# Writing each distance table to DRAM in two halves, in a two-layer attention and expert kernel

## The reference

```python
scores = jnp.einsum('bhqd,bhkd->bhqk', q, k) / scale
c2p_att = jnp.einsum('bhqd,hpd->bhqp', q, pos_k)
c2p = jnp.take_along_axis(c2p_att, c2p_pos, axis=-1)
p2c_att = jnp.einsum('bhkd,hpd->bhkp', k, pos_k)
p2c = jnp.swapaxes(jnp.take_along_axis(p2c_att, p2c_pos, axis=-1), -1, -2)
scores = scores + (c2p + p2c) / scale
probs = jax.nn.softmax(scores, axis=-1)
ctx = jnp.einsum('bhqk,bhkd->bhqd', probs, v)
```

## Time and profile before

| | |
|---|---|
| median of 3 runs | 2723.02 us (2717.69 to 2724.69) |
| the profiled execution | 2727.48 us |
| its span | 2725.4 us |
| mean granted clock of TensorE | 0.847 of full speed |
| busy share of the span | PE 72%, DVE 60%, ACT 38%, POOL 33% |
| DMA | 456.40 MB, mean 167 GB/s over the span |

### The profile page before, as it was taken

One profiled execution on the slowest core, in us unless ns is written; L12 is line 12 of the kernel. 1 busy time (PEld: TensorE's weight loads), 2 busy tenths in 40 slices (PEclk: granted clock), 3 DMA queues, 4 the chain that ended last, 5 costly groups with the idle time before them and its releaser, 6 DMA issues. The chain is left out here.

```text
span 2725.4 us, 47318 instructions
## 1 busy us (share of the span) xinstructions
PE 1965.8 (72%) x13556; PEld 1445.9 (53%) x13557; DVE 1632.0 (60%) x4103; ACT 1046.4 (38%) x2098; POOL 898.0 (33%) x1079
## 2 busy tenths in 40 slices
PE   6867777777777777777769999755335159999742
PEld 3435666666666666665646666433225028877421
DVE  8946665666666566665765553577747754444344
ACT  3445554555555555555423223332001163333000
POOL 4122222222222222222232220267630015554656
PEclk9979898998988888888979999777565559999876
DMA  4679998998999899999742110000001414447333
GB/s 149 195 238 287 278 290 262 290 280 271 284 266 281 255 281 269 276 280 282 233 122 62 48 30 1 0 0 0 0 19 47 178 32 155 154 148 139 109 97 110
DMA packets 290039, 456.40 MB, mean 167 GB/s; under 512 B 38608, under 2 KB 225024, under 8 KB 289824
## 3 DMA queue, kind: packets, MB, share of 16 engines
q1 hardware_dynamic: 269344, 398.77, 48.6%
q0 software_dynamic: 16320, 42.39, 6.3%
q10 hardware_dynamic: 4160, 12.58, 1.2%
HBM read 236.67 MB, written 216.92 MB: 166 GB/s over the span
## 5 line engine op out<-in xcount | busy, mean ns | idle before, releaser
L935 DVE CUSTOM_DVE_ANT_0 probs<-bank,c2p 128x512 f32<-128x512 f32 x512 | 351.8, 687 | 425.7 <-PE bank L832 217.9
L893 ACT ACTIVATE probs<-probs,neg_max 128x512 f32<-128x512 f32 x512 | 371.5, 726 | 69.9 <-DVE neg_max L935 69.5
L908 ACT COPY a_stage<-bank 128x320 f32<-128x320 f32 (+1 forms) x512 | 211.9, 414 | 427.1 <-PE bank L801 416.3
L944 DVE COPY probsT<-bank 128x512 f32<-128x512 f32 x512 | 351.2, 686 | 11.0 <-PE bank L842 10.6
L842 PE MATMUL bank<-ident,probs 128*128 128x128 f32 x2048 | 334.7, 289 | 1.0 <-ACT probs L893 0.9
L813 PE MATMUL bank<-tab,k 96*128 96x320 bf16 (+1 forms) x512 | 165.0, 322 | 197.1 <-DVE b_stage L887 149.6
L842 PEld LDWEIGHTS bank<-ident,probs 128*128 128x128 f32 x2048 | 277.3, 152 | 13.1 <-issue 1.8
L771 POOL COPY end_c2p<-a_stage 128x4 f32<-128x4 f32 (+1 forms) x128 | 24.8, 194 | 752.0 <-ACT a_stage L908 596.9
L2122 POOL DMA_INDIRECT p_x_tile<-y_d,p_token x160 | 153.0, 956 | 329.4 <-POOLq L1813 207.4
L832 PE MATMUL bank<-ident,p2c 128*128 128x128 f32 x1280 | 249.1, 296 | 0.0
L827 PE MATMUL bank<-k,q 96*128 96x384 bf16 (+1 forms) x512 | 167.3, 327 | 91.7 <-DMA p2c<-p2c_d 66.2
(11 more groups left out here) (254 smaller groups left out, 3770.0 us busy)
## 6 DMA issues: line engine op xcount, KB each, us to landing
p2c_d<-b_stage SPq DMA_DIRECT2D x64, 640.0 KB, 4.9
c2p_d<-a_stage SPq DMA_DIRECT2D x64, 640.0 KB, 4.5
p2c_d<-b_stage SPq DMA_DIRECT2D x64, 576.0 KB, 5.2
c2p_d<-a_stage SPq DMA_DIRECT2D x64, 576.0 KB, 3.5
p2c<-p2c_d SPq DMA_DIRECT2D x256, 144.0 KB, 4.5
c2p<-c2p_d SPq DMA_DIRECT2D x256, 144.0 KB, 4.3
o_sorted_d<-p_o_pair SPq DMA_DIRECT2D x80, 256.0 KB
k<-k_stack_d SPq DMA_DIRECT2D x192, 64.0 KB
```

Of the source, the lines that this page charges most:

```text
L893: act.activation(probs[:, w % 2, j, :], probs[:, w % 2, j, :], ACT.Exp, bias=neg_max[:, w % 2, j:j + 1], scale=-1.0).then_inc(exp_done, 1)
L908: act.copy(staged(a_stage, wa % 2, wa % TPB)[:, j, :], bank[A_BANK][:, 0:width(wa % TPB)]).then_inc(a_copied, 1)
L935: dve.tensor_tensor_reduce(probs[:, w % 2, j, :], bank[S_BANKS[(HB * w + j) % 3]][:], c2p[:, w % 2, j, :], -SCALE, LOWEST, ALU.add, ALU.mi ...
L944: dve.tensor_copy(probsT[:, wp % 2, j], bank[T_BANKS[j % 2]][:].rearrange("p (k q) -> p k q", k=TPB)).then_inc(probsT_copied, 1)
```

## The change

Each of the two writes of a step becomes two, with two batches each. The first half of table a waits for two copies in place of four, the first half of table b for one copy of DVE and one of ACT. SP's list in a step is now: first half of a, first half of b, second half of a, second half of b. The semaphores `a_written` and `b_written` now count 32 for a table, and every wait on them is adapted.

```diff
                         if is_unit(i2, w2):
                             kt = w2 % TPB
-                            sp.wait_ge(b_written[w2 % 2], 16 * (BODY // 2 * i2 + w2 // 2 + 1))
+                            sp.wait_ge(b_written[w2 % 2], 32 * (BODY // 2 * i2 + w2 // 2 + 1))
...
-                            sp.wait_ge(a_written[w1 % 2], 16 * (BODY // 2 * i1 + w1 // 2 + 1))
+                            sp.wait_ge(a_written[w1 % 2], 32 * (BODY // 2 * i1 + w1 // 2 + 1))
...
-                        if is_unit(ia, wa):
-                            sp.wait_ge(a_copied, HB * (BODY * ia + wa) + HB)
-                            sp.dma_start(written(c2p_d, wa), staged(a_stage, wa % 2, wa % TPB)).then_inc(a_written[wa % 2], 16)
-                        if is_unit(ib, wb):
-                            wait_count(sp, p2c_loaded[wb % TPB], 64 * (4 * ib + wb // TPB))
-                            sp.wait_ge(b_copied_dve, 2 * (BODY * ib + wb) + 2)
-                            sp.wait_ge(b_copied_act, 2 * (BODY * ib + wb) + 2)
-                            sp.dma_start(written(p2c_d, wb), staged(b_stage, wb % 2, wb % TPB)).then_inc(b_written[wb % 2], 16)
+                        for half in range(2):
+                            two = slice(2 * half, 2 * half + 2)
+                            if is_unit(ia, wa):
+                                sp.wait_ge(a_copied, HB * (BODY * ia + wa) + 2 * half + 2)
+                                sp.dma_start(written(c2p_d, wa)[:, two], staged(a_stage, wa % 2, wa % TPB)[:, two]
+                                             ).then_inc(a_written[wa % 2], 16)
+                            if is_unit(ib, wb):
+                                if half == 0:
+                                    wait_count(sp, p2c_loaded[wb % TPB], 64 * (4 * ib + wb // TPB))
+                                sp.wait_ge(b_copied_dve, 2 * (BODY * ib + wb) + half + 1)
+                                sp.wait_ge(b_copied_act, 2 * (BODY * ib + wb) + half + 1)
+                                sp.dma_start(written(p2c_d, wb)[:, two], staged(b_stage, wb % 2, wb % TPB)[:, two]
+                                             ).then_inc(b_written[wb % 2], 16)
```

More of the change, by code:

```diff
@@ L884, in copy_b @@
                     if j < 2:
-                        wait_count(eng, b_written[w % 2], 16 * (BODY // 2 * i + w // 2))
+                        wait_count(eng, b_written[w % 2], 32 * (BODY // 2 * i + w // 2))
                         wait_count(eng, b_ends_copied, m - 1)
@@ L905, in step @@
                                 if j == 0:
-                                    wait_count(act, a_written[wa % 2], 16 * (BODY // 2 * ia + wa // 2))
+                                    wait_count(act, a_written[wa % 2], 32 * (BODY // 2 * ia + wa // 2))
                                     wait_count(act, a_ends_copied, m - 1)
```

## The result

The changed kernel takes 2738.84 us (median of 5 runs, 2736.68 to 2748.83) against 2724.11 us (5 runs, 2717.69 to 2726.07): ratio 1.0068, 95% interval 1.0045 to 1.0092, so 12 to 25 us slower. Measured once more (experiment 6) the ratio was 1.0089 (1.0064 to 1.0114). The mean of the two, 1.0079, is +21 us. The forecast, no change with +3 us, had the wrong case: the change is slower. The time lies in the full range (2698 to 2772), which is wide enough to hold both slower rivals, and outside the 2716 to 2734 of the forecast itself.

The account below looks back on a forecast made before the run. The prediction took the attention stage to be paced by its transfers and the SP queue issuing them. Terms 13 + 4 - 14 = +3 us gave a median of 2726.0 us, range 2698 to 2772.

Parts of the forecast that it names:

- What bounds the stage: Attention stage, 1190 us for 128 units: paced by its transfers (DMA share 0.93) and the one queue, SP, issuing them.
- Term A: Table writes: halved pieces add transfer work, 0.2 us a unit, 26 us, of which half was counted: +13 us.
- that part is paced by SP: Stretch with only reads left: SP hands out a read each 0.46 us, so only half of 26 us was counted.
- the hold: Second p2c read after the writes, 1.20 us: said to wait until the first write is through, clocked from its issue.
- Term B: SP queue: a second pair of writes costs 1.0 to 1.1 us a unit, mostly covered while SP is held: +4 us.
- Term C: Where SP waits for a or b, first halves go out earlier; cap 70 us, priced at -14 us.
- Rival 1: SP queue becomes the bound: four writes fill it and later reads are held; +41 us, about 2764; chance 0.14.
- Rival 2: Transfer rate bounds, every added piece felt: +42 us, 2765; milder form 26 us less C, +12; chance 0.13.
- Rival 3: Head start worth its cap: half of 70 us returns through earlier c2p reads; -35 us, 2688; chance 0.20.
- Rival 4: In 78 of 128 units the first half starts when the whole did; 2723; chance 0.48 together with the forecast.
- The signs I named: New profile: SP's first-half waits nearly vanish, DMA share rises to 0.94 or 0.95, c2p wait changes under 20 us.
- bound of 15: Attention stage, 1190 us before: the prediction is wrong if it comes out under 1175 or over 1205.

Follow-up runs that it names:

- experiment 6: The changed kernel measured again, unchanged, against the kernel before on another chip: ratio 1.0089 (1.0064 to 1.0114).
- experiment 7: The changed kernel with the first halves of a and b issued ahead of the three loads of q or k: ratio to before 1.0059.
- experiment 8: The kernel before with the whole write of table a issued by ACT in place of SP: ratio 1.0027 (1.0004 to 1.0050).
- delay run: The kernel before with 16 extra semaphore instructions on SP, about 1.0 us, between the writes of a and b in every step: ratio 1.0049, +13 us.
- experiments 3 and 4: The kernel before, whole writes, with 32 or 256 bytes left free between batches 1 and 2, cutting each partition's piece in two: ratios 1.0127 and 1.0132.
- experiment 5: The changed kernel with both halves of a table waiting for all its copies, so no head start: ratios to before 1.0120 and 1.0106.
- experiment 9: The kernel before with each write split into two of 64 partitions with whole pieces, none ahead of its last copy: ratio 1.1142, +308 us.

## Why the forecast missed the case, point by point

- **What bounds the stage.** That the queue comes late and the head start is small was right: experiment 7 had to move the first halves ahead of the loads to give more of one. "Paced by its transfers and by the one queue" was half right. The DMA share fell with the change, and taking work from SP (experiment 8) brought nothing. The loop, as I read it from the waits, is: last copy of b, its write, eight reads, DVE, the next copies; only what lengthens it would cost. No run cuts that loop open.
- **Term A**, priced at +13 us after halving a price of 0.2 us a unit. The write rate fell from 410 to 395 GB/s, which is 0.11 us a unit and 15 us; subtraction of the delay run gives 17 to 19 us, with 9 of uncertainty; experiments 3 and 4 bound it from above at 34 to 36. The first two suggest that nearly all of the added transfer time is felt. That 13 came near them is luck: the transfer time was priced too high (26 us, measured 15; the stretch of 367 GB/s that stood for small pieces was a mixed one, 75% of its bytes the `ctx_raw` write) and then halved without a run that showed the half. The step that failed is the halving, "that part is paced by SP": the writes stand ahead of the held reads, and a write that ends later may end the hold later. That last link is argued: with whole writes and the delay the second read ends 3.8 us after the first write, with halves 4.1 (medians), which fits it and was not tested by itself.
- **Term B**, priced at +4 us: measured 13 by the delay alone (11 by the end of the stage), the largest of the three misses. The price uncovered, 1.0 us, was right: the first read starts 0.9 us later. There is a cover, and a second microsecond costs seven times the first. The step that failed is the mechanism of the cover: "clocked from that write's issue", and so "the third read starts where it started". The second read ends at a median of 3.5 us after the first write before, 3.8 with the delay and 4.1 with halves, so the hold gave back half of the added time and not all of it. It was read in three steps, at 3.2 to 3.3, where half of the steps before already ended it after 3.5. What covered most of the rest, SP's waits for a, b and GpSimd's fill (98.4 us before, 60.6 with the delay), was not counted as a cover.
- **Term C**, priced at -14 us: measured -9 by the times, with some 7 of uncertainty, and -13.5 by the end of the stage in two traces of each kernel. The price stands.
- **The sum.** 17 + 13 - 9 = +21 us, where 17 is what the mean of experiment 5 leaves over the delay run. It meets the measured mean (+21) by construction, since these numbers come from the same ratios; what is independent of it are the write rate's 15 us and the delay run's 13. I had 13 + 4 - 14 = +3. Every term was there; half of the miss is B.
- **Rivals.** Rival 1, the full queue as a bound, is out by its price (+41 us), not by its sign. It had named an end of the second read beyond 3.5 us, and with the change that is so in 112 of 115 steps (before, in 61 of 117). The second pair of writes is held too: the third and fourth write take 0.38 and 0.45 us to issue, the first two 0.35 (medians). That speaks for a queue that fills; that halves move the end more than the delay does fits both readings. Rival 2 in its milder form (26 us less C, +12) came nearest by its number, but 13 us of the cost are the queue's time, which it lacks. Rival 3 is out: of 70 us at most, 9 to 14 came back. DVE waits more for `c2p`, not less. Rival 4 is true in part: SP waited before only 60 of 256 writes of a, at most.
- **The signs I named.** SP's waits about halved, for a (49 to 28) and for b (21 to 11). Taken apart, those of a are 7.9 us at first halves, nearly gone as I had said, and at most 20.0 at second halves; at most, since the same view gives 17.6 us there in experiment 5, where a second half has nothing left to wait for. The share of DMA fell in place of rising. The stage grew by 14.6 us, a hair inside the bound of 15 that I had set for being wrong, which shows that bound to have been too wide for an effect of 0.3%.
- **The rule of the Trainium skill** (DMA: Bandwidth & Descriptors, Rules for kernel authors: coalesce small transfers) pointed the right way. The fixed time of 2 us per transfer, which that page fits for transfers issued by GpSimd, did not show as a cost here; the costs that did are 0.5 us of the issuing queue for each further transfer and 4% of the write rate. The same table advises against splitting a transfer by partition halves and says that the two serialize; experiment 9 agrees and is worse than that, 206 GB/s for 410.

No kernel here beat the one before. What stays open: what the hold is, in terms of the queue (a number of transfers, of pieces, or the moment of a landing); and the sharp size of A, for which the runs give 15 to 30 us.

## What to carry to other kernels

Splitting a write to start it earlier is worth something only if the queue that issues it gets there earlier: look first at what the issuing engine does when the half is ready. If one queue issues writes and the reads that follow them in a loop, measure the slack behind the writes with a pure delay of one and of two units; it tells whether a small addition is hidden and how near the edge is. A cover that is read in three steps of a timeline is to be counted over all steps before it goes into a sum. When terms of opposite sign are each near the resolution, add them without rounding any of them down for cover.

## What the runs showed of the hardware

- Two writes of 64 partitions move at 206 to 208 GB/s at a full DMA share, one of 128 partitions at 410, with the same pieces of 4608 and 5120 bytes.
- A write's issue on SP takes 0.35 us with 128 pieces and 0.52 us with 256, at the same bytes; one with 64 pieces of full size, from 64 partitions, takes 0.45 us (medians, of the first two writes of a step).
- Cutting the pieces of a write from 5120 and 4608 bytes to half takes the write rate from 410 to 395 GB/s; where the second piece starts (32 or 256 bytes on) did not matter (1.0127 and 1.0132).
- Reads issued behind two writes of 640 KB hold SP: the second takes 1.1 to 1.2 us in the three steps shown before the change, where an unheld one takes 0.43 to 0.50. It ends 3.5 us after the first write (median of 117 steps). With 1 us of delay between the writes it ends at 3.8, with the writes in halves at 4.1, and four reads then take 2.3 and 2.2 us in place of 2.8.
